# A macaron transformer block on one core: all sixteen experts for every token, or the four chosen ones gathered into tiles of 256 rows

## What is computed

```python
x = x + 0.5 * moe(LN(x))      # first FFN  ("f1")
x = x + attention(LN(x))
x = x + 0.5 * moe(LN(x))      # second FFN ("f2"), same weights
```

```python
yo = einsum('tei,ehi->teh', silu(g) * u, down_w)          # all experts
routed = einsum('te,teh->th', combine, yo)                 # combine is 0 for 12 of 16
```

## Time and profile before

| | |
|---|---|
| median of 3 runs | 2850.76 us |
| span of the profiled execution, first to last instruction | 2843.8 us |
| PE busy | 2728.3 us, 96% |
| DVE busy | 2065.1 us, 73% |
| ACT busy | 1263.1 us, 44% |
| POOL busy | 960.6 us, 34% |
| DMA | 30.07 MB, 11 GB/s over the span |
| mean granted TensorE clock | 0.991 |

### The profile page before, as it was taken

The page is one execution under the profiler, slowest core; times in us unless marked ns, Lnnn a source line. Parts: engine busy times, 40 slices in busy tenths (PEclk is TensorE's granted clock), DMA queues, the critical chain, the costliest instruction groups (busy, mean ns, idle before and its releaser), DMA issues.

```text
span 2843.8 us, 55213 instructions
## 1 busy us (share of the span) xinstructions
PE 2728.3 (96%) x18155; PEld 1699.2 (60%) x18155; DVE 2065.1 (73%) x5317; ACT 1263.1 (44%) x1890; POOL 960.6 (34%) x830
## 2 busy tenths in 40 slices
PE   8989999999999999999999999999999999999989
PEld 5555656656565665656656566565665656656555
DVE  6776867768677676776777777677786867768665
ACT  4454435354353544535445253443534435354342
POOL 2333333233332333333333342333423333233322
PEclk9999999999999999999999999999999999999999
DMA  4000000000000000000000000000000000000000
GB/s 127 31 1 1 16 2 9 9 1 16 2 16 2 1 16 2 16 2 1 16 2 16 2 1 16 2 16 2 9 9 2 16 2 9 9 1 9 1 8 8
DMA packets 29812, 30.07 MB, mean 11 GB/s; under 512 B 1590, under 2 KB 29516, under 8 KB 29516
## 3 DMA queue, kind: packets, MB, share of 16 engines
q1 hardware_dynamic: 29328, 26.22, 2.9%
q10 hardware_dynamic: 188, 0.03, 0.0%
HBM read 17.85 MB, written 8.39 MB: 9 GB/s over the span
## 4 chain that ended last, share of the span: by engine, by line
PE 84%; issue 6%; ACT 4%; DVE 4%; POOL 1%; DMA 0%; DVEq 0%; ACTq 0%; POOLq 0%; SPq 0%
PE bank L483 20%; PE bank L484 20%; PE bank L485 20%; PE bank L540 7%; PE bank L538 7%; PE bank L539 7%; PE bank L512 2%; DVE prod L990 1%; ACT soft L758 1%; PE bank L545 1%; PE bank L546 1%; PE bank L547 1%; ACT L726 1%; DVE xn L897 1%; ACT silu_g L726 1%
## 5 line engine op out<-in xcount | busy, mean ns | idle before, releaser
L822 POOL TENSOR_TENSOR h_lo<-prod,h_hi 128x512 f16<-128x512 f32 x576 | 666.9, 1158 | 1759.2 <-ACT h_hi L732 1758.7
L483 PE MATMUL bank<-xt_hi_f,gu_hi 128*128 128x512 f16 x2304 | 883.5, 383 | 52.0 <-issue 32.5
L484 PE MATMUL bank<-xt_lo_f,gu_hi 128*128 128x512 f16 x2304 | 883.3, 383 | 0.0
L485 PE MATMUL bank<-xt_hi_f,gu_lo 128*128 128x512 f16 x2304 | 883.1, 383 | 0.0
L990 DVE SCALAR_TENSOR_TENSOR prod<-bank,silu_g 128x512 f32<-128x512 f32 x576 | 396.2, 688 | 642.4 <-PE bank L485 425.2
L732 ACT ACTIVATE h_hi<-prod 128x512 f16<-128x512 f32 x576 | 362.9, 630 | 1036.6 <-DVE prod L990 1007.5
L539 PE MATMUL bank<-dn_lo,h_hi 128*128 128x256 f16 x2048 | 558.3, 273 | 0.0
L540 PE MATMUL bank<-dn_hi,h_lo 128*128 128x256 f16 x2048 | 558.3, 273 | 0.0
L538 PE MATMUL bank<-dn_hi,h_hi 128*128 128x256 f16 x2048 | 558.3, 273 | 0.0
L726 ACT ACTIVATE silu_g<-bank 128x512 f32<-128x512 f32 x576 | 343.0, 595 | 481.7 <-PE bank L485 476.1
L979 DVE SCALAR_TENSOR_TENSOR x<-bank,comb_f,x 128x256 f32<-128x256 f32 x1024 | 423.9, 476 | 6.8
(11 more groups left out here) (158 smaller groups left out, 3037.5 us busy)
## 6 DMA issues: line engine op xcount, KB each, us to landing
x<-in_attn_x_dram SPq DMA_DIRECT2D x16, 512.0 KB, 3.5
out_dram<-xo SPq DMA_DIRECT2D x16, 512.0 KB, 3.6
act<-in_ffn_gate_w_dram SPq DMA_DIRECT2D x16, 128.0 KB, 2.5
act<-in_ffn_up_w_dram SPq DMA_DIRECT2D x16, 128.0 KB, 2.8
act<-in_ffn_down_w_dram SPq DMA_DIRECT2D x8, 256.0 KB, 2.9
act<-in_attn_k_w_dram SPq DMA_DIRECT2D x2, 256.0 KB, 3.1
act<-in_attn_q_w_dram SPq DMA_DIRECT2D x2, 256.0 KB, 2.8
act<-in_ffn_sh_gate_w_dram SPq DMA_DIRECT2D x2, 128.0 KB, 2.2
```

Of the source, the lines that this page charges most:

```text
L483: pe.matmul(out_ap, a_hi, b_hi, start=(i == 0), stop=False)
L484: pe.matmul(out_ap, a_hi, b_lo, start=False, stop=False)
L485: last = pe.matmul(out_ap, a_lo, b_hi, start=False, stop=(i == n - 1))
L822: pool.tensor_tensor(h_lo[:, e % 3], prod[:, e % 2], h_hi[:, e % 3], ALU.subtract).then_inc(lo_done, 1)
```

## The change

The two FFNs of all sequences are now worked through in four stages: first FFN of sequences 0 to 7 and 8 to 15, second FFN of the same halves (`CHUNKS = (8, 8)`; a routing r is one sequence's FFN, 0 to 15 the first, 16 to 31 the second). In each routing, the router gives every token four slots in regions of a DRAM buffer, one region per expert; POOL writes the normed rows there with indirect DMAs (scatter). When a stage's routings are done, a table of tiles of 256 rows is computed, each with its expert's number and its row. A pair of tiles is one unit of gate and up. The results go to a second DRAM buffer, and POOL gathers four rows for each token, which DVE adds up. The shared experts are computed as before. An order of all pieces in half steps is computed in Python (`Plan.build`), and each engine walks the same list, without a hardware loop.

```diff
+SLOT = 256
+ROW = 2 * D
+CHUNKS = (8, 8)
+RING_X = 3
+RING_W = 8
+RING_G = 4
+RING_Y = 4
+RING_YG = 4
+def stages():
+    for ffn in range(2):
+        first = SEQS * ffn
+        for n in CHUNKS:
+            tiles = (n * TOK * TOPK + E * (SLOT - 1)) // SLOT
+            tiles += tiles % 2
...
+class Plan:      # build(): one gate or up per half step h, while there is a unit
+                if second_shared is not None:
+                    unit, second_shared = second_shared, None
+                elif shared_next < 2 * SEQS and shared_ready.get(shared_next, never) <= h and weights > 3:
+                    unit, second_shared = ("shared", shared_next, 0), ("shared", shared_next, 1)
+                elif pair < n_tiles // 2 and turned >= 2 * pair + 2:
+                    unit = ("pair", pair)
...
+                period = dict(head=12 if 0 in ready else 6, body=14, tail=9 if pair < n_tiles // 2 else 4)[kind]
+                late = dict(head=0, body=done.get(self.stage_of(n), never),
+                            tail=done.get(self.stage_of(SEQS + n), never))[kind]
...
         @block.sync
+            def turn_tab(q):
+                for e in range(E):
+                    row = sp.value_load(ends[0:1, q, e:e + 1], ...)
+                    sp.dma_start(xd[q][bass.ds(row, SLOT), :], zeros[:, :])
+            def xload(t):
+                row = sp.value_load(tab_at(t, 2), min_val=0, max_val=E * stage[q]["region"])
+                sp.dma_start(xg[:, t % RING_G], xd[q][bass.ds(row, SLOT), :].rearrange("(p j) c -> p j c", j=2))
+            def ystore(t):
+                row = sp.value_load(tab_at(t, 1), min_val=0, max_val=rows_of[q] - SLOT)
+                sp.dma_start(yd[q][bass.ds(row, SLOT), :]..., ybuf[:, t % RING_Y].bitcast(U32))
         @block.tensor
+            def trans(t):       # 2 parts x 2 halves x 2 blocks, float16
+                            last = pe.transpose(ps16[:, at:at + P], xg[:, t % RING_G, j, ...], ident16[:])
+            def w_of(tensor, e, m, k):
+                return tensor[:, bass.ds(e, 1), m, k].rearrange("p e o -> p (e o)")
+            def gate_or_up(g, m, ps):
+                for a, t in enumerate(unit_tiles(g)):
+                    if m == 0:
+                        expert_of[t] = pe.value_load(tab_at(t, 0), min_val=0, max_val=E - 1)
+                    last = three(ps[:, c], [(w_of(gu_hi, expert_of[t], m, k), w_of(gu_lo, expert_of[t], m, k),
+                                             xp[:, k], xp[:, KT + k]) for k in range(KT)])
+            def down(key):      # one bank; one tile, or half of a shared unit
+                        w_hi, w_lo = (w[:, bass.ds(e, 1), :]... for w in (dn_hi, dn_lo))
         @block.scalar
+            def xev(t):         # 128x1024 float16 from PSUM
+                act.activation(xtp[:, pair % 2, ...], turn_ps[:].bitcast(F16)..., ACT.Copy)
+            def yev(t):         # 128x512 from PSUM
+                act.activation(flat(ybuf[:, t % RING_Y]), down_ps[:], ACT.Copy)
         @block.gpsimd
-                    pool.tensor_tensor(h_lo[:, e % 3], prod[:, e % 2], h_hi[:, e % 3], ALU.subtract)
+            def scatter(key):
+                for k in range(TOPK):
+                    pool.indirect_dma_start(out=xd[q][:, :], out_offset=...idx[:, r % SEQS, t, k:k + 1]...,
+                        in_=xs[:, r % 2, t]...)                # 128 rows of 1 KB
+            def gather(key):
+                for j in range(TOPK):
+                    pool.indirect_dma_start(out=yg[:, t, j]..., in_=yd[q][:, :],
+                        in_offset=...idx[:, c % SEQS, t, j:j + 1]...)    # 128 rows of 1 KB
         @block.vector
+            def hilo(g):
+                dve.tensor_tensor(h_lo[:, g % 3], sp_g[:, g % 2], h_hi[:, g % 3], ALU.subtract)
+            def route_slots(r):    # slots from rank counts by PE, idx, and the four weights
+            def shared_sum(key): ...
+            def combine(key):      # 16 adds of 128x256 per routing, from SBUF
```

More of the change, by code:

```diff
@@ L105, in macaron @@
[L105 to L112, removed]
+        upto = sb("upto", [P, E, E])
+        numbers = sb("numbers", [P, 3 * E], I32)
+        expert = sb("expert", [P, E])
+        slot_steps = sb("slot_steps", [P, E])
+        tile_no = sb("tile_no", [P, 1])
+        tile_row = sb("tile_row", [P, 1])
@@ new lines, in stay_of_sum, with rows, stay_loaded, slot_uses @@
+        def stay_of_sum(c):
+            return nth("load", ("C1", c) if c < SEQS else ("C2", c - SEQS))
+        def rows(st):
+            return xb[:, st % RING_X]
+        def stay_loaded(engine, st):
+            engine.wait_ge(xb_loaded[st % RING_X], 16 * (st // RING_X + 1))
+        def slot_uses(t, ring):
+            return [(t - i) // ring + 1 if t >= i else 0 for i in range(ring)]
+        def unit_tiles(g):
+            kind, i = plan.units[g][:2]
+            return (2 * i, 2 * i + 1)
@@ L422, in quarters, with tab_at, shared_over @@
+        def tab_at(t, column):
+            q = plan.stage_of_tile(t)
+            i = t - stage[q]["tile"]
+            return tab[0:1, q % len(CHUNKS), column, i:i + 1]
+        def shared_over(r):
+            return plan.units.index(("shared", r, 1)) + 1
+        unit_of_pair = {u[1]: g for g, u in enumerate(plan.units) if u[0] == "pair"}
+        def quarters(n, b, ot):
             for half in range(2):
@@ L477, in _, with three @@
+            for i in range(RING_X):
+                sp.wait_ge(xb_stored[i], 16 * ((plan.count["load"] - i - 1) // RING_X + 1))
         @block.tensor
         def _(pe):
-            def three(out_ap, pairs):
+            def three(out_ap, pairs, more=False):
                 n = len(pairs)
@@ L575, in finish, with rank @@
-            def finish(stage, f):
-                down(f, E)
-            def project_in(n, i, p, routed):
+            def rank(r):
+                pe.wait_ge(route_step, ROUTE_STEPS * r + ROUTED_AT)
+                side_is_free(pe, "rank", r)
+                ps = side("rank", r)
+                pe.matmul(ps[:, 0:(TT + 1) * E], earlier16[:], mask[:].rearrange("p t e -> p (t e)"), start=True, stop=False)
+                for s in range(1, TT + 1):
+                    last = pe.matmul(ps[:, s * E:(TT + 1) * E], ones16[:],
+                                     mask[:, 0:TT + 1 - s].rearrange("p t e -> p (t e)"), start=False, stop=(s == TT))
+                last.then_inc(rank_done, 1)
```

1518 lines of the change are left out of this document (919 added, 599 removed).

## The result

The changed kernel took **3270.5 us** (median of 4 runs, 3265.8 to 3275.7) against 2849.8 us of the kernel before: 1.148 times the time, 95% interval 1.146 to 1.151. The forecast was 2320 us with a range of 2000 to 2800 and 0.12 for slower. Both the size and the side were wrong.

A forecast was written before the change was run, and what follows sets the result against it. PE's matmul stream was taken to bound the kernel. Heads 250, stage 0 360, bodies 1216, stage 3 290, last tails 170 and fills 30 made 2316 us of span, so 2320 us, range 2000 to 2800.

The forecast's parts named there:

- sum: Whole kernel: predicted stretches along the plan added up, 2316 us of span, for a time of 2320 us.
- heads: Half steps 0 to 65, no tiles: eight routings at DVE's pace with waits, start, weights, table and landing, 250 us.
- stage 0: Half steps to 173: 40 pairs at 7 us with the other eight routings at 9.7 us, 360 us.
- stage 3: Half steps 434 to 513: 40 pairs at 7 us beside eight tails, 290 us.
- last tails: Kernel's end: 128 gathers at 1.2 us on POOL, the last sum, a load and a store, 170 us.
- the 530 forecast: Whole kernel: the 1373 us of PE matmuls saved were to become some 530 us of gain.
- The bodies' factor of 1.2: Half steps 174 to 433, 16 sequences' sums and attention with 80 pairs: 1.2 times busiest engine, 1216 us.
- My 76 us per body: Each of 16 sequences' sum and attention, with its share of pairs: from 1.2 times ACT's sum, 1216 us for all.
- A pair: Two expert tiles on PE: 4.8 us of stream, taken as 7 us with register addressing, loads and waits.
- Rival 2: PE's sequencer binds everywhere through register-addressed weights, 10.6 us per pair, 2780 us in all; chance 0.22.
- Rival 3: POOL's queue of 1024 indirect DMAs binds and the kernel is slower, 3200 us at 3.1 us each; chance 0.12.
- The fills' 30 us: SP's 16 tail fills per stage sit ahead of tile loads and stores; pairs wait in two of four stages, 30 us.

The follow-up runs named there:

- group 5: Experiments on one chip where signals came in time; the changed kernel, unaltered, took 2796.1 us there, the kernel before 2849.9 us.
- no_both: Changed kernel without its 512 gathers and 512 scatters, so no indirect DMA at all; tiles loaded from fixed rows: 2646.7 us.
- no_both_fixed: Changed kernel without any indirect DMAs, and with PE taking expert weights by fixed addresses instead of loaded expert numbers: 2478.7 us.
- prefetch: Changed kernel with PE loading the next pair's expert numbers early, ahead of the waits: 2643.7 us on a chip with signals in time.
- paced_three_chunks: Changed kernel with indirect DMAs spread and paced, expert numbers loaded early, and three chunks per expert pass instead of two: 2602.8 us, ratio 0.913.
- no_both_fixed_fill: Kernel without indirect DMAs and with fixed expert addresses (2478.7 us), plus six extra 512-column matmuls ahead of each of 224 units: 2528.9 us.
- the void test: Changed kernel with gathers still indirect but indices 0 to 127 in order; 2791.1 us, compared with runs on another chip.
- paced: Changed kernel with each group's 16 indirect DMAs spread over 7 half steps instead of 4, POOL waiting for PE ahead of each: 2922.6 us.

## Why the prediction was wrong

The stages by the trace, in us. "Late" is the changed kernel's first profile, "in time" that of group 5, whose span is 479 us shorter.

| | sum | late | in time | no_both | no_both_fixed | prefetch |
|---|---|---|---|---|---|---|
| heads | 250 | 332 | 278 | 276 | 275 | 275 |
| stage 0 | 360 | 501 | 416 | 409 | 345 | 370 |
| bodies | 1216 | 1835 | 1583 | 1577 | 1555 | 1563 |
| stage 3 | 290 | 423 | 334 | 322 | 240 | 252 |
| last tails | 170 | 182 | 184 | 60 | 62 | 182 |

**The term that turned the sign was not in the sum.** The sum has the indirect DMAs cost POOL's own time and their landings; what they do to the signals between the other engines was put at nothing, without a reason. The same text took 479 us more where signals are late: 10.6 per group of 16 DMAs in stage 0, 11.1 in stage 3, 7.9 in the bodies, 6.8 in the heads, nothing in the last tails, where PE has no part. `no_both` agrees from the other side: but for its last gathers it is within 30 us of the changed kernel in time. The kernel before starts no DMA from POOL, and its trace could not show it. The size lies in the chip or in what surrounds it: in three of the five groups of experiments, each on a chip of its own, signals were late, in two they were not. Where signals come in time, the change makes the kernel 1.9% faster by one time beside seven of before; where they are late it is 15% slower. The 2796.1 us would have been inside the range by 4 us, and that would have been luck: the gain is 54 us, a tenth of the 530 forecast.

**The bodies' factor of 1.2 was mis-sized**, the largest error on either kind of chip: 1583 us in time against 1216. The prediction took the busiest engine, ACT at 1013, as the base; against it the bodies took 1.56 times. ACT and DVE have even less to do than it added up, 879 us against 1013 and 919 against 960. What it had too small is the waiting between the engines. Measured in these stretches (columns: stretch, its length, busy time and instructions of PE, PEld, DVE, ACT, POOL, clock, DMA share, GB/s):

```profile
692.00:1326.00 634.00, 471.70 (x3873) 358.78 (x3871) 362.98 (x860) 383.47 (x517) 230.61 (x234) 0.88 0.37 119
1326.00:1583.00 257.00, 136.74 (x922) 89.18 (x920) 156.16 (x408) 105.25 (x135) 107.46 (x108) 0.75 0.27 84
1583.00:2279.00 696.00, 506.28 (x4182) 387.14 (x4181) 399.62 (x1008) 389.96 (x533) 228.83 (x234) 0.87 0.37 118
```
```profile
L1447 DVE TENSOR_TENSOR kv<-bank,blockmask x16: 424/425/426, 800.2 to 2147.3; 128x256 f32<-128x256 f32 x16
```

The middle row is the stretch with hardly a pair. No engine is busy for more than 61% of it, yet the mask of K and V (L1447), once a body, comes every 81 to 83 us there and every 88 to 94 with pairs beside it; the 15 distances make 1347 us, 90 each. Without scatters and gathers they are the same 81 to 94, with fixed expert addresses too. So the floor is the body itself: 14 half steps of short pieces that wait for each other across three engines in one fixed order. One such wait, in the middle stretch:

```profile
1339.85 0.63 ACT L1009 ACTIVATE h_hi<-sp_g 128x512 f16<-128x512 f32 x1 [6.53 <-DVE sp_g L1379]
...
1350.50 0.69 DVE L1384 TENSOR_TENSOR h_lo<-sp_g,h_hi 128x512 f16<-128x512 f32 x1
...
1351.29 0.37 PE L704 MATMUL bank<-dn_hi,h_hi 128*128 128x256 f16 x1 [11.77 <-issue]
```

ACT has h_hi ready at 1340.48, but DVE does routing, attention and the weighted adds first and comes to h_lo 10.0 us later, and PE's `down`, which waits for it, starts after 11.77 us of idle time. In the stretch's other two bodies h_lo comes 10.0 and 15.5 us after h_hi. An engine that is busy for 61% holds up the others by its order. My 76 us per body came from an engine's sum, when the row to take was the length of the chain, to be added up from the body's own pieces. That pairs are cheap beside it (10 to 12 us for five or six) is what `paced_three_chunks` used: it has pairs beside all bodies, whose 15 distances make 1394 us.

Two small slips stand in the working of this term: the adds from SBUF were priced at 0.40 us and take 0.48, and ACT's 33 and 7.4 us make 40.4 per body, not 40.8.

**A pair** was taken at 7 us. In stage 3, in time, the median distance from the silu of one pair to that of the next is 8.8 us; by fixed addresses, without indirect DMAs, 6.15; with the load moved 6.5. The 2.2 us that I put on the registers is what fixed addresses gave back (8.4 to 6.15 between `no_both` and `no_both_fixed`), but the working was wrong twice. The stream doesn't run at 4.8 without them: PE waits for `xtp`, as this group of stage 3 of `no_both_fixed` shows (x304 of its 320 are recorded in the stretch from 2175 to 2415 us):

```profile
L701 PE MATMUL bank<-xtp,gu_hi 128*128 128x256 f16 x304 | 83.2, 274 | 44.0 <-ACT xtp L998 44.0
```

And arithmetic is not the cost: `prefetch` issues the same 320 loads and 3520 register operations, only the loads stand ahead of the waits instead of behind them, and gives back nearly all. The row of the load:

```profile
L794 PEldq TENSOR_LOAD <-tab x320: 295/303/1317, 337.3 to 3079.8; - x160
```

0.30 us in the median. With the register operation and the bounds check behind it, PE's first gate matmul of a pair follows the start of the load by 0.75 us in the median of stage 3, and a second load stands between the two tiles of a pair; the 0.9 taken for each was near. The Trainium skill, DMA: Bandwidth & Descriptors, section Latency and other measured facts, names a floor of some 600 ns for a `tensor_load`. The measurement decides: half of that. Rival 2 (10.6 us a pair) fell with it.

**POOL.** Taken 1.2 us, measured 1.0, and 1.26 from start to start in a group. Rival 3 was on the right side with a wrong mechanism: its price c came out at a third of 3.1, and POOL is 34% busy. The Trainium skill, SBUF — State Buffer, section SBUF: two separate sides, says that POOL can't write descriptors while DVE has the shared port. No run here shows that this matters: POOL's instructions are as long on a chip with late signals as on one without.

**What held.** The heads (250 against 278) and the last tails (170 against 184) in time, and the bytes: 382.95 MB against 380, hidden. The fills' 30 us could not be told apart.

**The clock.** 0.787 granted in the mean, 0.832 in time, where 0.9 had been named as what would prove the forecast wrong. It falls where PE waits: 0.75 in the stretch in which PE is busy for 137 of 257 us. It follows the waits. Whether it also lengthens them is open: an estimate from the distances of PE's float16 matmuls, 0.43 us in place of 0.216 for 512 columns at the lower level, is 25 us in that stretch and some 125 in all of the bodies, of the 367 by which they were over the sum. `no_both_fixed_fill` won nothing by more matmuls, but it left the clock of that stretch at 0.77 and its three bodies as long as before, 81 to 83 us.

**What stays open.** Why signals are late on some chips. Shown is: only beside indirect DMAs; not for plain DMAs of the same packets from the same queue, on a chip where the scatters' are late; less when they are spread; on chips 4, 7 and 13 and not on 5 and 9, with each chip seen once. Whether it is the chip, the time or a neighbour's load was not tried. Nor was the recording of the trace ruled out. Where signals are late, more than half of the records of the indirect DMAs' own increments are missing too, even in the last tails (400 of 2048 are there), where no time was lost. Each run on record has a span and a granted clock of its own, and none is known to have been taken without the profiler. The order of the rows was not tried again after the void test. And of the two paced versions with the early load neither ran on a chip with late signals, so that they beat the kernel before is shown only where signals come in time; `paced` alone took 2922.6 us against 2844.3 of the kernel before where they are late.

## What to carry to other kernels

When a plan interleaves a long chain of short pieces with bulk work, cost a period by the chain's own latency across the engines and compare that with the busiest engine; take the larger, and count the stretch in which the bulk work has run out. Put a register load ahead of the waits, while the queue behind it is still full: here that alone was worth 99 us on one chip, and 152 between two chips with signals in time. If a profile of a one-core program names "remote" or "another core" as the releaser, compare the increments with the ends of the instructions that make them, take a time without the profiler if there is a way, and run the kernel itself again beside each group of experiments, on each chip, before believing a difference.

## What was not expected of the hardware

- Semaphore increments of PE reached the others 7.5 and 11.2 us behind the end of their instruction in the group shown, while indirect DMAs were under way. Over 2 us late were 237 to 252 in the five profiles of kernels with all 1024 of them in groups on chips with late signals, 1 to 3 in the three such profiles on two other chips, and by the stricter count of the section on the result 195 to 225 and none. The same kernel took 3276.5 us and 2796.1 us, while the kernel before stayed between 2837 and 2857 in every group.
- An indirect DMA of 128 rows held POOL for 1.0 us and a plain one for 0.54, for the same packets.
